# Stacks of q and k that go through DRAM: one store and six loads in place of twelve transfers inside SBUF

## What is computed

```
x = x + layernorm(attention_1(layernorm(x)))       # 16 heads of 32, causal, rotary table
h = x' + attention_2(rmsnorm(x'))                  # x' = layernorm(x); low-rank q, k, v; half of each head rotated
y = h + experts(rmsnorm(h))                        # one shared expert, top 2 of 7 routed
out = x + layernorm(y)

attention: scores = q @ k.T * 32 ** -0.5, causal mask, softmax, @ v, @ w_o
```

## Time and profile before

| | |
|---|---|
| time before, median of 2 runs | 2734.35 us (2733.12 to 2735.57) |
| the profiled execution, its own time | 2744.92 us |
| its span | 2743.2 us |
| mean granted clock of PE | 0.929 of full speed |
| PE busy | 2309.2 us, 84% of the span |
| DVE, ACT, POOL busy | 1531.9, 1038.3, 618.1 us |
| attention stages | about 47 to 1911 us of the span, 64 groups |
| transfers `stacks<-parts` | 768 of 128 KB, median 2.8 us from issue to landing |

### The profile page before, as it was taken

How to read it: one execution, slowest core, us unless ns; L and a number is a source line. 1 busy time by engine, 2 the same in 40 slices (tenths; PEclk the granted TensorE clock), 3 DMA queues, 4 the chain that set the end, 5 groups by cost and what they waited for, 6 DMA issues and landing times. The chain is left out here.

```text
span 2743.2 us, 40006 instructions
## 1 busy us (share of the span) xinstructions
PE 2309.2 (84%) x14016; PEld 1570.2 (57%) x14016; DVE 1531.9 (56%) x4168; ACT 1038.3 (38%) x2164; POOL 618.1 (23%) x921
## 2 busy tenths in 40 slices
PE   4899988989888899988899898898599899999800
PEld 3565555655555565655656655454377688888600
DVE  2555556555565655556555565664455465555377
ACT  0234453333444332444433344443323155555400
POOL 1123221222322122223121231311232200000075
PEclk9999999999999999999899999998699899999955
DMA  5243344543344443444534434332454555555397
GB/s 158 62 118 106 108 137 118 147 108 93 108 126 144 116 124 93 112 130 114 155 93 118 117 97 133 92 84 72 162 193 176 197 197 198 209 190 193 139 325 270
DMA packets 228437, 386.24 MB, mean 141 GB/s; under 512 B 24718, under 2 KB 108558, under 8 KB 222606
## 3 DMA queue, kind: packets, MB, share of 16 engines
q1 hardware_dynamic: 157710, 290.87, 35.5%
q10 hardware_dynamic: 60288, 59.25, 6.6%
q0 software_dynamic: 10240, 33.56, 3.3%
HBM read 141.90 MB, written 140.51 MB: 103 GB/s over the span
## 5 line engine op out<-in xcount | busy, mean ns | idle before, releaser
L801 DVE CUSTOM_DVE_ANT_0 unused<-score,mask 128x128 bf16<-128x128 f32 (+3 forms) x1024 | 463.4, 486 | 415.3 <-PE score L979 404.7
L621 ACT ACTIVATE probs<-scoresT 128x512 f32<-128x512 f32 (+3 forms) x1024 | 409.5, 436 | 686.5 <-PE scoresT L1002 682.5
L979 PE MATMUL score<-stacks 96*128 96x256 f32 (+2 forms) x1024 | 382.4, 416 | 86.3 <-DMA stacks<-parts 75.6
L1002 PE MATMUL scoresT<-stacks 97*128 97x256 f32 (+2 forms) x1024 | 376.5, 417 | 28.0 <-ACT probs L621 12.4
L979 PEld LDWEIGHTS score<-stacks 96*128 96x128 f32 x1024 | 181.8, 194 | 270.1 <-issue 167.9
L555 POOL TENSOR_SCALAR_AFFINE_SELECT probs<-probs 128x512 f32<-128x512 f32 x256 | 163.0, 637 | 640.0 <-ACT probs L621 640.0
L814 DVE RECIPROCAL total<-total 128x128 f32<-128x128 f32 x256 | 233.8, 934 | 79.8 <-ACT whole L632 73.2
L909 PE MATMUL middle<-wqkv,XT 128*128 128x128 f32 x2048 | 268.0, 279 | 6.8 <-ACT XT L588 5.9
L909 PEld LDWEIGHTS middle<-wqkv,XT 128*128 128x128 f32 x2048 | 260.1, 194 | 19.1 <-ACT XT L588 7.7
L1002 PEld LDWEIGHTS scoresT<-stacks 97*128 97x128 f32 x1024 | 186.6, 197 | 123.1 <-ACT probs L621 77.3
L1031 PE MATMUL middle<-wo,outT 128*128 128x512 f32 x512 | 254.8, 599 | 1.4 <-DVE parts L783 1.4
(11 more groups left out here) (173 smaller groups left out, 3749.5 us busy)
## 6 DMA issues: line engine op xcount, KB each, us to landing
stacks<-parts SPq DMA_DIRECT2D x768, 128.0 KB, 2.8
x_slots<-mask ACTq DMA_DIRECT2D x56, 1024.0 KB, 6.8
xr<-x_slots SPq DMA_DIRECT2D x22, 1024.0 KB, 6.0
y_slots<-y SPq DMA_DIRECT2D x22, 1024.0 KB, 4.3
raw<-in_gates SPq DMA_DIRECT2D x23, 512.0 KB
raw<-in_ups SPq DMA_DIRECT2D x23, 512.0 KB
raw<-in_downs SPq DMA_DIRECT2D x23, 512.0 KB
normed<-in_L_attn_x SPq DMA_DIRECT2D x8, 1024.0 KB, 7.7
```

The source lines that it names most:

```text
L621: act.activation(probs[:, m % 2, h, 0:width], scoresT[:, u % ST_BANKS, first:first + width], ACT.Exp, scale=SCALE).then_inc(exp_done, 1)
L801: ins = dve.tensor_tensor_reduce(unused[:, t, 0:width], score.bank(name)[:, first:first + width], mask[:, T - width:T], 1.0, MASKED, ALU.a ...
L979: ins = pe.matmul(score.bank(name)[:, first:first + width], heads[0:ROWMAX, 0, h, t * P:(t + 1) * P], heads[0:ROWMAX, 1, h, 0:width], star ...
L1002: pe.matmul(scoresT[:, u % ST_BANKS, 0:T - first], heads[0:ROWMAX + 1, 1, h, j * P:(j + 1) * P], heads[0:ROWMAX + 1, 0, h, first:T], start ...
```

## The change

SP no longer copies from `parts` to `stacks` directly. For group n it stores all of `parts` (1024 KB) into a DRAM tensor `parts_kept[n % 2]` by one transfer, waits until that has landed, and then issues six loads of 256 KB: for each of the three slots and each of the two sides, one part of all four heads, partition 32 h + d of the DRAM tensor going to partition 32 s + d, head h. All six count on the semaphore of head 0, and PE waits for the full count before every head. ACT, before it overwrites `parts`, waits for the store only.

```diff
-        PER_STACK = 3 * 16
+        PER_STACK = 6 * 16
+        parts_stored = semaphore("parts_stored")
...
                     if n >= STACKS:
                         sp.wait_ge(st_filled, GH * TT * (n - STACKS + 1))
-                    for h in range(GH):
-                        for s, chosen in enumerate((slice(0, 2), slice(2, 0, -1), slice(0, 4, 3))):
-                            sp.dma_start(stacks[n % STACKS][s * HD:(s + 1) * HD, :, h, :].bitcast(F32),
-                                         parts[h * HD:(h + 1) * HD, chosen, :].bitcast(F32))\
-                              .then_inc(stacked[n % STACKS][h], 16)
+                    kept = parts_kept[n % 2]
+                    sp.dma_start(kept, parts[:, :, :].bitcast(F32)).then_inc(parts_stored, 16)
+                    sp.wait_ge(parts_stored, 16 * (n + 1))
+                    for s, chosen in enumerate(((0, 1), (2, 1), (0, 3))):
+                        for side, part in enumerate(chosen):
+                            sp.dma_start(stacks[n % STACKS][s * HD:(s + 1) * HD, side, :, :].bitcast(F32),
+                                         kept[:, part, :].rearrange("(h d) t -> d h t", h=GH))\
+                              .then_inc(stacked[n % STACKS][0], 16)
...
                     if n > 0 and which == 0:
-                        for h in range(GH):
-                            act.wait_ge(stacked[(n - 1) % STACKS][h], PER_STACK * ((n - 1) // STACKS + 1))
+                        act.wait_ge(parts_stored, 16 * n)
...
                     if part == 0:
-                        pe.wait_ge(stacked[n % STACKS][h], PER_STACK * (n // STACKS + 1))
+                        pe.wait_ge(stacked[n % STACKS][0], PER_STACK * (n // STACKS + 1))
...
+    parts_kept = [nc.dram_tensor(f"parts_kept{n}", (P, 4, T), F32, kind="Internal").ap() for n in range(2)]
```

More of the change, by code:

```diff
@@ L272, in score_fills, with attention_layers @@
             yield step, *which
-def attention_layers(nc, x, weights, tables, ln1_w, x1_out, xin_kept, h_out, x_slots, blocks):
+def attention_layers(nc, x, weights, tables, ln1_w, x1_out, xin_kept, h_out, parts_kept, x_slots, blocks):
     w_qkv, w_o, kv_d, q_d, k_u, v_u, q_u, rope_k, rope_q, o_w = weights
@@ L1950, in build @@
                                                  "rope_q_w", "o_w")],
-                     (a["rope1"], a["rope2"]), a["L0_ffn_ln1_w"], *kept, slots[0], blocks)
+                     (a["rope1"], a["rope2"]), a["L0_ffn_ln1_w"], *kept, parts_kept, slots[0], blocks)
     summed = nc.dram_tensor("h_summed", (blocks, T, D), F32, kind="Internal").ap()
```

## The result

The changed kernel takes 3374.93 us (median of 2 runs, 3370.13 to 3379.73) against 2734.35 us. The ratio is 1.2336, 95% interval 1.2301 to 1.2372: 23% slower. The profiled execution has a span of 3368.4 us at a mean granted clock of 0.854.

The account below looks back on a forecast made before the run. PE, in order and busy 84% of the span, was taken to bound the kernel with its stalls. A longer path (420 us) plus clock (net 110 us) put 530 us on 2734.35, giving 3264 us; range 3060 to 3400.

Parts of the forecast that it names:

- rival B: Store to DRAM comes in behind the zeros, landing after 7.7 us in 56 groups: 95 us more, 3359 us; chance 0.15.
- the forecast's own bounds: Path of 14 to 15.6 us and clock cost of 1.4 to 2.8 us a group: 3180 to 3355 us.
- PE is in order and sets the end: Attention stages: their end is PE's own work plus its stalls; a held-up matmul holds all behind it.
- The store: 1024 KB from `parts` to DRAM, a new link in front: lands after 6.0 us with zeros, 4.3 without.
- The loads: Six loads into 32 partitions each: 8.5 us from first issue to last landing, bounds 5.7 and 9.7.
- The path: From last part to first score: 14.7 us with zeros, 13.0 without; 420 us more over all groups.
- All heads on one semaphore: PE's first head waits for all six loads, before for three of twelve transfers; heads 1 to 3 gain nothing.
- ACT's release and SP's second wait: ACT's copy waits for the store, worth nothing; SP's wait holds little beyond the loads, some row transfers.
- The clock: PE's clock falls in each stop and stays low behind it: 2.1 us a group, 134 us, net 110.
- Rival C: PE's clock costs nothing more, since the long stops lie outside the work: 3154 us; chance 0.05.
- A: Six loads run at their issues' pace, path 11.9 us with zeros and 10.2 without: 3076 us; chance 0.18.
- D: Not slower: few large transfers clear the jam behind the zeros, whole stack there before PE, 2648 us; chance 0.02.

Follow-up runs that it names:

- e6_wide_target: Changed kernel with its six loads sent to a buffer over all 128 partitions, stacks holding a constant, so without true scores: 3180.60 us.
- e9_parts_apart: Changed kernel with the DRAM tensor laid out part by part, so each load reads one whole stretch and the store writes 2 KB pieces: 3336.54 us.
- e10_half_loads: Changed kernel with each load cut in two, giving twelve loads of 128 KB by part, all on one semaphore: 3324.55 us.
- e1_one_sem: Kernel before the change, its twelve transfers inside SBUF all on one semaphore, so every head waits for all twelve: 3131.64 us.
- e5_pe_kept_busy: Changed kernel with 12 needless PE matmuls a group ahead of the wait for head 0's stack: 3312.09 us.
- e8_dram_by_head_zeros_later: Changed kernel with twelve loads by head, a semaphore for each head, and the zeros half a group later: 2800.26 us.

## Why the prediction was right, and where it wasn't

The side and the mechanism were right: the first score of every group waits for the stack, the wait isn't covered by anything, and the clock adds to it. The forecast was 3264 us, 111 too low. The measured 3375 lies in the range, but above the 3355 of the forecast's own bounds: the range holds it because it was drawn over rival B, whose mechanism did not occur, and that part is luck. Nor do those bounds, 14 to 15.6 us of path, follow from the terms: with 5.7 and 9.7 us for the loads the paths with zeros are 11.9 and 15.9. By its own steps:

*PE is in order and sets the end.* Held. The attention stages grew by 636 us: 531 of d and 105 of the rest. In all ten other kernels, too, time follows these two sums.

*The store.* Forecast 6.0 us with zeros, measured 4.0 at the median and 4.2 on average. Here the choice of a middle was wrong: zeros and store are issued in the same instant and the store's packets go first. That speaks against rival B, though its 3359 us is the number nearest to the result; its mechanism isn't what happened. The Trainium skill's rule that the engines take the queues in turn (DMA: Bandwidth & Descriptors, Queues, rings and completion order), which carried B, did not show in this trace: until 1335.85 the store had 77.7% of the engines and the zeros 1.2%. Whether the zeros' packets were not there yet, or had to wait, the trace doesn't show.

*The loads.* This is the term that was mis-sized. Forecast 8.5 us from the first issue to the last landing; measured 12.0 with zeros and 10.3 without. 1.7 of the 3.5 missing are the zeros, which the forecast had charged to the store and which fall on the first load. The two errors of about 1.7 us cancel in the sum, which is luck; the remaining 1.8 is more than the forecast allowed for, since 10.3 lies over its upper bound of 9.7. These 1.8 are the rate and the first landing: I had taken the old transfers' 6.6 us for the bytes and 1.9 around them, but the first 256 KB from DRAM land after 4.0 us and the next at 1.2 to 1.3 us each. By e6_wide_target the 32 partitions of the target cost 2.7 us a group, but that was foreseen in kind: the 6.6 us were themselves of transfers into 32 partitions. Why loads from DRAM came in slower than those was not tested beyond e9_parts_apart and e10_half_loads.

*The path.* 14.7 with zeros and 13.0 without, measured 16.4 and 14.8; 111 us more over 64 groups, which is the miss.

*All heads on one semaphore.* The prediction had the direction (head 0 waits for all) but gave it no price of its own; it was inside the path. e1_one_sem gives it 300 of the 531 us, so this step was worth most.

*ACT's release and SP's second wait.* Held at nothing beyond the store's own landing: SP sat 251.4 us in that wait, but the loads and stores of rows behind it made no engine wait longer. PE's wait for the normalized rows is 35.0 us at DVE and 11.6 at ACT (35.5 and 11.8 before), though the load `normed` lands after 13.1 us for 7.7.

*The clock.* Forecast 110 us net, measured 105 as growth of the rest; e5_pe_kept_busy takes 131 off, for the 134 that the forecast had before it netted what stood there already. Rival C is out. The sign named for it missed: a mean clock near 0.90 was forecast, and 0.85 came. About half of the 761 us at the lower level lie inside the stops, where PE has nothing to do; while PE is busy they rise from some 145 us to 387, and that rise of 242, at the forecast's own 2.8 us for 6.8, makes the 100 us that were seen.

*Rivals A and D.* A needed the loads at the pace of their issues; they were slower, not quicker, than taken. D had nothing for it, and e8_dram_by_head_zeros_later shows that even the best form stays over the time before.

## What to carry to other kernels

Where an engine works in order, price a transfer by how soon its first consumer can start, not by its bytes or its count: the same twelve transfers behind one common semaphore took 14% longer than with a semaphore for each head at the same landing of the last. Look at what else is issued in the same instant: a write that nobody awaits, moved by half a group, was worth 3.6% in the kernel before. And an exposed stop of PE costs more than its length, since the clock falls in it and is still low behind it: 531 us more of d took 105 more with them.

## What the runs showed of the hardware

A store of 1024 KB from 128 partitions in pieces of 8 KB landed after 4.0 us, with another 1024 KB in pieces of 1 KB issued 0.02 us ahead on ACT's queue (the group shown under the result); there the two did not take turns, the store's packets ran first. The same bytes in pieces of 2 KB (e9_parts_apart) took 4.6 at the median. Of the loads that follow the store, in groups without zeros, the first 256 KB into 32 partitions landed after 4.0 us, into 128 partitions after 3.2. Twelve loads of 128 KB by head had their last landing 10.1 us after their first issue, six of 256 KB by part 11.8. Of this difference of 1.6 us (before rounding) the layout in DRAM alone takes 1.0 off the six loads, at 0.5 more for the store, the size of a load alone takes 0.7 off, and the other order of the targets nothing.
